# Two-layer kernel, second layer: the first half of the convolution over four units in place of five

## What is computed

```python
xz = gn(x) @ in_proj_w.T;  xv, z = split(xz)          # 256 channels each
xc = silu(depthwise_conv3x3(xv) + conv_b)             # 9 taps, 256 channels
# windows of 8 x 8 pixels, four scan orders k; two windows are merged into one sequence of 128
x_dbl = einsum('bkdl,kcd->bkcl', xs, x_proj_w)        # -> dts (8), B (16), C (16)
dt = softplus(dt_projs_w @ dts + dt_projs_b)
h = h * exp(dt * A) + dt * u * B;  y = sum_n h * C    # 16 states per channel, scanned along the sequence
y = layernorm(y + Ds * xs, back in pixel order) * silu(z)
out = x + y @ out_proj_w.T
```

## Time and profile before

| | us |
|---|---|
| median of 3 runs | 26914.43 |
| lowest, highest | 26913.54, 26918.26 |
| the profiled execution, its own time | 26905.02 |
| its span, first to last instruction | 26903.2 |
| VectorE busy | 24918.8 (93%) |
| ScalarE busy | 23843.2 (89%) |
| GpSimd busy | 23340.4 (87%) |
| TensorE matmuls, weight loads | 21633.7 (80%), 16468.8 (61%) |

### The profile page before, as it was taken

One profiled execution on the slowest core, in us unless ns is written; L12 is line 12 of the kernel. 1 busy time (PEld: TensorE's weight loads), 2 busy tenths in 40 slices (PEclk: granted clock), 3 DMA queues, 4 the chain that ended last, 5 costly groups with the idle time before them and its releaser, 6 DMA issues.

```text
span 26903.2 us, 494637 instructions
## 1 busy us (share of the span) xinstructions
PE 21633.7 (80%) x144686; PEld 16468.8 (61%) x144686; DVE 24918.8 (93%) x23263; ACT 23843.2 (89%) x49162; POOL 23340.4 (87%) x10372
## 2 busy tenths in 40 slices
PE   5997788888888788888888888888888878888887
PEld 1775566666666666666666666666666666666666
DVE  6777899999999999999999999999999999999999
ACT  5886789999999999999999999999999999999998
POOL 4000799999999999999999999999999999999999
PEclk8998899999999999999999999999999999999999
DMA  4113333333333333333333333333333333333333
GB/s 160 53 53 116 122 108 108 107 108 107 109 107 108 107 107 110 107 107 108 109 107 106 109 108 107 109 106 108 109 108 107 109 108 107 109 107 109 107 109 97
DMA packets 2198523, 2870.18 MB, mean 107 GB/s; under 512 B 696026, under 2 KB 965882, under 8 KB 2195194
## 3 DMA queue, kind: packets, MB, share of 16 engines
q1 hardware_dynamic: 2186586, 2803.33, 34.6%
q10 hardware_dynamic: 9216, 33.82, 0.3%
HBM read 2667.01 MB, written 169.74 MB: 105 GB/s over the span
## 4 chain that ended last, share of the span: by engine, by line
ACT 34%; PE 25%; issue 16%; DVE 11%; POOL 2%; ACTq 1%; DVEq 1%; POOLq 0%
DVE hst L1576 10%; ACT dAs L1443 8%; ACT dbT L1465 8%; PE yps L1281 8%; ACT dA L1443 6%; PE misc L1182 5%; PE dbx L1266 5%; PE misc L1201 2%; ACT vab L1398 2%; DVE hc L1584 1%; PE misc L1218 1%; ACT dbx L1443 1%; ACT vab L1384 1%; PE cps L1243 1%; ACT dtuT L1455 1%
## 5 line engine op out<-in xcount | busy, mean ns | idle before, releaser
L1639 POOL TENSOR_TENSOR dbu<-dtu,bb 128x1024 f32<-128x1024 f32 x4096 | 9699.9, 2375 | 995.6 <-DVE hst L1576 987.1
L1576 DVE TENSOR_TENSOR_SCAN hst<-dA,dbu 128x1024 f32<-128x1024 f32 x4096 | 9346.8, 2282 | 515.7 <-ACT dA L1443 439.0
L1653 POOL TENSOR_TENSOR hc<-hst,cc 128x1024 f32<-128x1024 f32 x4096 | 9738.2, 2377 | 6.1 <-DVE hst L1576 4.6
L1281 PE MATMUL yps<-ident,hc 128*128 128x128 f32 x65536 | 8805.0, 280 | 416.2 <-POOL hc L1653 339.7
L1281 PEld LDWEIGHTS yps<-ident,hc 128*128 128x128 f32 x65536 | 7829.0, 145 | 1550.1 <-issue 895.0
L1576 DVE TENSOR_TENSOR_SCAN hst<-dAs,dbx 128x1024 f32<-128x1024 f32 x3584 | 8119.1, 2265 | 124.1 <-issue 66.5
L1266 PE MATMUL dbx<-ident,dbT 128*128 128x128 f32 x28672 | 4089.2, 289 | 3080.4 <-DVE hst L1576 2754.2
L1465 ACT ACTIVATE dbT<-dtuT,bT 128x256 f32<-128x256 f32 x14336 | 6124.7, 495 | 18.2
L1266 PEld LDWEIGHTS dbx<-ident,dbT 128*128 128x128 f32 x28672 | 3340.1, 147 | 4426.6 <-DVE hst L1576 3376.3
L1443 ACT ACTIVATE dA<-dtv,aneg 128x508 f32<-128x508 f32 x8192 | 5288.7, 678 | 394.7 <-DVE hst L1576 389.0
L1443 ACT ACTIVATE dAs<-dtv,aneg 128x508 f32<-128x508 f32 x7168 | 4741.0, 710 | 390.9 <-DVE hst L1576 390.8
(11 more groups left out here) (188 smaller groups left out, 25163.8 us busy)
## 6 DMA issues: line engine op xcount, KB each, us to landing
bb<-l_bscr SPq DMA_DIRECT2D x1024, 1024.0 KB, 5.8
cc<-l_bscr SPq DMA_DIRECT2D x1024, 1024.0 KB, 5.7
bx<-l_bscr SPq DMA_DIRECT2D x1024, 256.0 KB, 6.2
xg<-xgp SPq DMA_DIRECT2D x512, 85.0 KB, 2.3
xgp<-hst ACTq DMA_DIRECT2D x64, 516.0 KB, 6.6
xt<-in_x_dram SPq DMA_DIRECT2D x128, 256.0 KB, 2.8
l_xnT<-xo SPq DMA_DIRECT2D x128, 256.0 KB, 2.0
xn<-l_xnT SPq DMA_DIRECT2D x256, 128.0 KB, 2.2
```

The costliest lines, as they stand in the source:

```text
L1281: mm = pe.matmul(yps[:, p, f * P:(f + 1) * P], hc[:, u % HB, f * 512 + p * P:f * 512 + (p + 1) * P], ident[:], is_transpose=True, start=fi ...
L1576: nc.vector.tensor_tensor_scan(hst[:, v % 4, way], decays.rearrange("p f c -> p (f c)")[:, way], inputs.rearrange("p f c -> p (f c)")[:, way],
L1639: nc.gpsimd.tensor_tensor(to, dtu[:, step % 2], row.unsqueeze(1).to_broadcast([P, 2, 512]), ALU.mult).then_inc(s_inp, 1)
L1653: nc.gpsimd.tensor_tensor(hc[:, v % HB].rearrange("p (f c) -> p f c", f=2), hst[:, v % 4].rearrange("p (f c) -> p f c", f=2), row.unsqueez ...
```

## The change

The cuts of the convolution's first half are moved. Before, units 11, 12, 13, 14 and 15 issued taps 0-1, 2-3, 4-5, 6-7 and 8. Now units 11, 12, 13 and 14 issue taps 0-1, 2-4, 5-6 and 7-8. `JOBS` has no entry for unit 15 any more. The last piece is now the job of unit 14, so ScalarE copies it at the end of the pair of 14, where before it copied it after the first decay of the pair of 16. The order of the filling jobs is unchanged, and so are all their counts.

```diff
-        TAPS = ((0, 2, 4, 6, 8, 9), (0, 2, 3, 4, 5, 6, 7, 8, 9))
+        TAPS = ((0, 2, 5, 7, 9), (0, 2, 3, 4, 5, 6, 7, 8, 9))
         for f, u in enumerate((11, 24)):
             for t in range(len(TAPS[f]) - 1):
                 JOBS[u + t] = ("pre", "conv", f, t)
```

## The result

The kernel after takes 27174.85 us (median of 3 runs, 27157.85 to 27175.99) against 26914.43: a ratio of 1.0094, with an interval of 1.008 to 1.0108, so 260 us slower. The forecast was 27023 us, and its range ended at 27070. The direction was right; more than half of the loss was not in the sum. The profiled execution is 27174.85 us itself, its span 27173.0 us.

A forecast was written before the change was run, and what follows sets the result against it. It took TensorE's queue (units 12 to 17), then GpSimd's (from unit 24), as limits; 126 x 0.86 = 108 us on 26905.0 gives 27013, plus 9.4 for the median of runs: 27023 us, +0.40%, range 26960 to 27070.

The forecast's parts named there:

- its slack of 3.02 us: GpSimd between inputs(20) and inputs(28): 3.02 us of a 23.92 us stretch could absorb lateness from the rstd.
- the 108 of the sum: Whole kernel: 126 blocks, each 0.86 us late from scan(30) on, add 108 us.
- the last of the sum: TensorE's side job behind GpSimd's product of unit 19: slips a few tenths more than VectorE, near or below 0.86; counted nothing.
- the predicted road: Late rstd delay GpSimd, inputs(28) starts 0.86 us late, and scan(30) waits for GpSimd's dbu, 0.86 us a block.
- one of my signs of being wrong: GpSimd's gap before inputs(28) was expected to close; finding it still open would show the prediction wrong.
- The third tap hidden: TensorE's units 12 to 14 have air, GpSimd's slack takes all lateness: no change, 26914 us; chance 0.09.
- VectorE's road alone: GpSimd has some 0.3 us more slack; only VectorE's 0.56 us a block remains: 71 us, 26985 us; chance 0.14.
- my 0.56: VectorE at scan(21): delay left after part of scan(18)'s 1.08 us is given back, 0.56 us a block.
- Late scan(18) kept: Decays of 20 and 21 slip too, so scan(18)'s 1.08 us is not given back: 136 us, 27050 us; chance 0.10.
- The copy free of its wait: Last tap done when ScalarE reaches the copy; scans 20 and 21 stop waiting: 76 us faster, 26839 us; chance 0.07.

The follow-up runs named there:

- the third tap alone: Kernel before with tap 4 moved into unit 12, still five units and the copy where it was: 26933.47 us, ratio 1.0007.
- the zeros: Kernel after with two zero matmuls of 512 columns on TensorE ahead of unit 19's sum: 27104.78 us, ratio 1.0069.
- the reordered kernel: Kernel before with four units (0-1, 2-3, 4-5, 6-8), unit 16's spread before unit 14's taps, unit 18's before the x-projection, unit 15's sum behind it: 26872.61 us.
- both kernels with zeros: Kernel after with zero matmuls ahead of unit 19's sum: eight of 128 columns, 27569.22 us; two of 512 columns, 27104.78 us.
- the `rstd` first: Kernel after with the two small rstd instructions moved ahead of the copy in the pair of 14: 26944.12 us, ratio 1.0008.
- the copy in the pair of 16: Kernel after with ScalarE's copy moved back behind the decay of 18, in the pair of 16: 26941.89 us, ratio 1.0009.
- all of TensorE's new order: Kernel before, cuts and copy kept, with spreads of 16 and 18 ahead of unit 14's taps and the x-projection, unit 15's sum behind it: 26922.04 us.
- the spread first: Kernel before with only the spread of unit 16 moved ahead of the taps of unit 14 on TensorE: 26949.9 us, ratio 1.0005.
- the third tap in unit 14: Kernel after with cuts 0-1, 2-3, 4-5, 6-8, the third tap in unit 14 in place of unit 12: 27189.62 us, ratio 1.0099.

## Why the prediction was wrong

**Right, and shown.** TensorE's queue sets the spreads (the third tap alone delays them). ScalarE's order puts `rstd` 3.87 us late (3.88 predicted), GpSimd carries it, its slack of 3.02 us is used up, and where TensorE keeps its clock, 0.86 us a block arrive at scan(30): 0.87 in the 32 blocks at full clock, 0.88 with the zeros. If TensorE had kept it everywhere, the loss would have been 126 x 0.87 = 110 us, against the 108 of the sum.

**Wrong.** The step that failed is the last of the sum, on TensorE's sum of unit 19: "so that job slips by a few tenths more than VectorE, still by less than 0.86 or near it; I count nothing for it." The time of that product was right to 0.02 us. At full clock the slip was right too: in the 32 blocks the side job is 0.98 us late against VectorE's 0.38, and `dtv` does not wait. What I did not ask is what TensorE does while it waits. It is idle for 2.09 us, comes back at half clock in 92 of 124 blocks, and there the side job is 1.61 us late on the mean and ScalarE's first step behind the `dt` matmuls (`vab`) 2.09 us, so that `dtv` waits: 66.20 - 64.75 = 1.45 us more, 1.45 x 92/124 x 126 = 136 us. The term that I put at nothing measures 136 us.

This also takes the predicted road away in those 92 blocks. VectorE itself is then later than GpSimd's 0.86 us, GpSimd waits for it before `inputs(28)`, and scan(30) hardly waits. An open gap at that place was one of my signs of being wrong, and it is open in the 92: GpSimd's `dbu` waits for VectorE's scans 777.5 us in all, before 987.8, with the gap of `inputs(22)` gone everywhere and that of `inputs(28)` in the 32 only. So the split into 110 and 136 us compares blocks with and without half clock; the two losses do not arrive one after the other in a block. Together they are 246 of the 260 us; the rest is spread over small changes at other places of the block, whose cause I did not try. The windows carry the granted clock, and 0.97 from 13976 to 14043 says that it does fall in places; the forecast read them for busy shares only.

**Rivals.** The third tap hidden: false, and the rule of the Trainium skill that would give it (Perfetto Trace Analysis, Identifying the Most-Contended Engine) speaks of where to look for headroom, not of who is queued behind whom; the third tap delays units 15 and 16 by 0.53 us together, though VectorE has it back by unit 17, so that the tap alone costs nothing that can be told. VectorE's road alone (26985): false, by `inputs(28)` and scan(30); VectorE's own delay at scan(21), 0.38 us on the mean, was below my 0.56: in the block shown the decay of 21 is 0.39 us late, and scans 20 and 21 stand 2.22 us apart, not 2.29. Late scan(18) kept: false, it is given back. The copy free of its wait: false as the change stands; the reordered kernel is that rival made true, with 61 us where I had worked out 76.

**Open.** The 32 blocks that keep full clock have the same pause in front of the sum as the 92, 2.07 to 2.11 us, so its length is not all that decides. Over the runs the number of blocks with half clock there does follow it: none of 124 with 0.37 us or less (both kernels with zeros) and none with 0.85 and 0.59 us with the sum between (the `rstd` first, the copy in the pair of 16); 4 and 20 with one pause of 1.32 us (before, the third tap alone); 5, 13 and 23 with 1.55 us (all of TensorE's new order, the spread first, the reordered kernel); 92 and 94 with 2.09 us (after, the third tap in unit 14); 102 with 2.42 us; 118 with 3.30 us. In the runs with 1.55 us or less no scan(24) was late. What tips a single block was not settled. That the gaps in unit 3 come from the longer loop body is argued from where and when they appear; no run changed the body's length with nothing else.

## What to carry to other kernels

When a piece of work is moved in an engine's written order, look for small instructions behind it that another engine waits for: here 0.4 us of `rstd` behind a copy carried nearly all of 260 us, and moving them ahead gave nearly all of it back. When an engine comes late, follow it to TensorE as well, and ask how long TensorE then has nothing at all to do: two pauses of 0.85 and 0.59 us with work between were harmless, one of 2.09 us cost half its clock in three blocks of four, just where a result was due. A stall seen in the waits is worth its time only if the next one behind it is moved as well.

## What the hardware showed that I had not expected

- In the block shown, after a pause of 2.09 us in TensorE the granted clock was 0.50 for the next 2 us and 0.68 for the 2 us after; eight transposing matmuls took 1.97 us in place of 1.09. The clock fell in 92 of 124 blocks; in the other 32, after the same pause, it stayed. Eight records of zero matmuls in the pause kept it at full clock in all 124 blocks. That a TensorE without work is throttled to half its clock is stated in the Trainium skill (TensorE: Matmul & The Clock Gate, Part 1: The HAM clock gate); the trace agrees in the 92 blocks, with the 0.50 above, while in the other 32 the same pause left it at 1.00.
- With more instructions in the body of the block loop, time was lost at another place, for which the length of the body is the likely cause but not a shown one: with 32 more records TensorE stood for 4.18 us, released by nothing that is recorded, after the loop's turn, and the block lost 4.08 us in unit 3; with 8 more it lost 0.53, of which up to 0.24 also appears with no instruction added. The added matmuls themselves lay in idle time.
